# Two mixtures of experts in a decoder stack: the sorted blocks run as one pipeline over all parts

## The reference

```
# layer 0: the two best of eight experts, gated by silu
logits = x @ router_weight;  pick the 2 largest, weights from softmax
y = sum over the 2 picks of  weight * ((silu(x @ w1a[e]) * (x @ w1b[e])) @ w2[e])
x = layernorm(x + y)

# layer 1: one expert (best group of four, best expert of its two)
h = relu(x1 @ w1[e] + b1[e]);  y = combine * (h @ w2[e] + b2[e])
# then the layer's own norm with scale and bias, a residual, and the outer layernorm
```

## Time and profile before

| | us |
|---|---|
| median of the runs (three) | 4633.01 |
| the profiled execution | 4642.58 |
| its span, first to last instruction | 4640.8 |
| PE busy | 3776.7 (81%) |
| DVE busy | 3217.5 (69%) |
| ACT busy | 2241.0 (48%) |
| POOL busy | 1622.7 (35%) |
| mean granted TensorE clock | 0.897 of full |

### The profile page before, as it was taken

How to read it: one execution, slowest core, us unless ns; L and a number is a source line. 1 busy time by engine, 2 the same in 40 slices (tenths; PEclk the granted TensorE clock), 3 DMA queues, 4 the chain that set the end, 5 groups by cost and what they waited for, 6 DMA issues and landing times. The chain is left out here.

```text
span 4640.8 us, 137309 instructions
## 1 busy us (share of the span) xinstructions
PE 3776.7 (81%) x48696; PEld 2762.1 (60%) x48696; DVE 3217.5 (69%) x7860; ACT 2241.0 (48%) x4080; POOL 1622.7 (35%) x2677
## 2 busy tenths in 40 slices
PE   8997995268819999899998474898998968879986
PEld 6775664145517777677676352676775434447665
DVE  7986884233338888788796226788887767759985
ACT  4554551023424444466685133555784355545543
POOL 5653434603451111122354413233222234435543
PEclk9998995578969999999997687899999978889998
DMA  2011112165510000011001463000111100000001
GB/s 71 27 46 35 37 37 78 47 178 158 155 52 2 0 0 0 24 42 43 15 16 35 128 167 88 14 13 13 33 32 47 52 7 0 0 12 23 23 17 37
DMA packets 293801, 209.56 MB, mean 45 GB/s; under 512 B 51136, under 2 KB 272192, under 8 KB 293440
## 3 DMA queue, kind: packets, MB, share of 16 engines
q1 hardware_dynamic: 233760, 157.72, 11.9%
q0 software_dynamic: 12288, 25.19, 1.8%
q10 hardware_dynamic: 47520, 23.60, 1.7%
HBM read 122.49 MB, written 54.53 MB: 38 GB/s over the span
## 5 line engine op out<-in xcount | busy, mean ns | idle before, releaser
L955 POOL DMA_INDIRECT L0f_YG<-L0f_sorted_y,L0f_IDY x128 | 124.7, 974 | 214.8 <-DMA L0f_sorted_y<-L0f_YB 177.6
L1356 DVE TENSOR_TENSOR L0f_G<-L0f_SG,L0f_psH 128x512 f32<-128x512 f32 x106 | 73.0, 689 | 158.7 <-ACT L0f_SG L1098 95.2
L2219 POOL TENSOR_TENSOR L1a_rs<-L1a_ag,eps 128x1 f32<-128x1 f32 x64 | 12.3, 192 | 475.0 <-DVE L1a_ag L2379 475.0
L936 POOL DMA_INDIRECT L0f_sorted_x<-X,L0f_IDX x128 | 123.5, 965 | 86.7 <-DVE L0f_IDX L1202 48.6
L1029 PEld LDWEIGHTS L0f_psO<-L0f_WB,L0f_G 128*128 128x128 f32 x848 | 109.5, 199 | 57.1 <-issue 56.5
L1362 DVE TENSOR_TENSOR L1m_YB<-L1m_psO,L1m_WB 128x512 f32<-128x512 f32 x37 | 25.4, 687 | 170.4 <-PE L1m_psO L1029 115.6
L1029 PE MATMUL L0f_psO<-L0f_WB,L0f_G 128*128 128x128 f32 x848 | 111.6, 282 | 24.9 <-issue 24.6
L1022 PE MATMUL L1m_psH<-L1m_XT,L1m_WB 128*128 128x512 f32 x148 | 85.8, 709 | 55.8 <-ACT L1m_G L1101 40.0
L2306 PE MATMUL L1a_psO<-L1a_WO,L1a_OT 128*64 128x128 f32 x2048 | 125.9, 276 | 6.4 <-ACT L1a_OT L2330 5.0
L2240 PE MATMUL L1a_psF<-L1a_XT,L1a_WQ 128*128 128x256 f32 x512 | 130.1, 388 | 0.5 <-DVE L1a_KT L2195 0.5
L955 POOL DMA_INDIRECT L1m_YG<-L1m_sorted_y,L1m_IDY x64 | 62.7, 980 | 189.7 <-DMA L1m_sorted_y<-L1m_YB 148.1
(11 more groups left out here) (684 smaller groups left out, 12971.8 us busy)
## 6 DMA issues: line engine op xcount, KB each, us to landing
L0f_WB<-in_w12a SPq DMA_DIRECT2D x53, 312.0 KB
L0f_XB<-L0f_sorted_x SPq DMA_DIRECT2D x53, 256.0 KB
L0f_sorted_y<-L0f_YB ACTq DMA_DIRECT2D x53, 256.0 KB
L1m_WB<-in_w12b SPq DMA_DIRECT2D x37, 321.0 KB
L1m_XB<-L1m_sorted_x SPq DMA_DIRECT2D x37, 256.0 KB
L1m_sorted_y<-L1m_YB ACTq DMA_DIRECT2D x37, 256.0 KB
L0f_sorted_x<-L0f_AC SPq DMA_DIRECT2D x27, 256.0 KB, 2.6
L1m_sorted_x<-L1m_AC SPq DMA_DIRECT2D x27, 256.0 KB, 2.9
```

Of the source, the lines that this page charges most:

```text
L936: nc.gpsimd.indirect_dma_start(out=sorted_x[p][:, :], out_offset=bass.IndirectOffsetOnAxis(ap=IDX[:, k, t:t + 1], axis=0), in_=X[:, t, :], ...
L955: nc.gpsimd.indirect_dma_start(out=YG[:, b % 4, k, t % TB, :], out_offset=None, in_=sorted_y[p][:, :], in_offset=bass.IndirectOffsetOnAxis ...
L1356: nc.vector.tensor_tensor(G[0:f, J % 2, c, :], SG[0:f, c, :], up, ALU.mult).then_inc(S["g_ready"].sem, 1)
```

## The change

`PARTS` is set inside `routed_experts` and is 32, 16, 16 for layer 1 (blocks 15, 11, 11; still 37). The engines no longer empty the pipeline between parts: SP asks for rows(J+3) in every case, TensorE turns J+1 and does second(J−1) across the boundary, ScalarE likewise. The fills of part p+1 are issued one for each of the first eight blocks of part p. The side rows of batches 0 to 7 are asked for at every second block of part 1 (J = 15, 17, ..., 29) and worked on two blocks later (17 to 31); those of batches 8 to 15 come after the blocks, each behind a mixing step. The steps now stand so. Layer 0: 25:0, 27:1, 30:2, 32:3, 42:4, 44:5, 47:6, 49:7, 52:8, and eight after the blocks. Layer 1: 18:0, 20:1, 22:2, 24:3, 26:4, 28:5, 30:6, 32:7, 34:8, 36:9, and eight after.

```diff
-        PARTS = (16, 32, 16)
-
         def routed_experts(L, top, weights, router, bias=None, XO=None):
             gated, NE, GT = top == 2, 8, 16
+            PARTS = (16, 32, 16) if gated else (32, 16, 16)
...
-            step_after = {}
+            step_after, at = {}, 0
             for p in parts[1:]:
-                for k in range(PARTS[p - 1] // TB):
-                    at = first[p] + (4 + 2 * k if gated else 3 + 3 * k // 2)
-                    if at < first[p + 1]:
-                        step_after[at] = part_tile[p - 1] // TB + k
+                at = max(at, first[p] + ((10, 4)[p - 1] if gated else 3))
+                for b in range(part_tile[p - 1] // TB, part_tile[p] // TB):
+                    if at < BLOCKS:
+                        step_after[int(at)] = b
+                    at += 2.5 if gated else 2
+            SIDES = NBATCH // 2
...
-                    def fill(p):
+                    def fill(p, e):
                         made(sp, "prep", p + 1)
-                        for e in range(NE):
-                            last = sp.value_load(BT[0:1, p, 2, e:e + 1], min_val=0, max_val=ROWS - BATCH)
-                            sp.dma_start(rows_at(sorted_x[p], last), AC2[:, 0]).then_inc(S[f"filled{p}"].sem, 16)
-
-                    fill(0)
+                        last = sp.value_load(BT[0:1, p, 2, e:e + 1], min_val=0, max_val=ROWS - BATCH)
+                        sp.dma_start(rows_at(sorted_x[p], last), AC2[:, 0]).then_inc(S[f"filled{p}"].sem, 16)
+
+                    for e in range(NE):
+                        fill(0, e)
...
                     for J in range(BLOCKS):
-                        if J in (2, 6):
-                            fill((2, 6).index(J) + 1)
+                        p, k = part_of[J], J - first[part_of[J]]
+                        if p + 1 < len(PARTS) and k < NE:
+                            fill(p + 1, k)
                         if J + 3 < BLOCKS:
-                            if part_of[J + 3] == part_of[J]:
-                                rows(J + 3)
+                            rows(J + 3)
                             expert(J + 3)
-                        if J + 1 < BLOCKS and part_of[J + 1] != part_of[J]:
-                            for k in range(J + 1, J + 4):
-                                rows(k)
-                        if gated and J < NBATCH:
-                            side_rows(J)
+                        if gated and p == 1 and k % 2 == 0 and k // 2 < SIDES:
+                            side_rows(k // 2)
+                    if gated:
+                        for b in range(SIDES, NBATCH):
+                            side_rows(b)
...
                     for J in range(BLOCKS):
-                        if J + 1 < BLOCKS and part_of[J + 1] == part_of[J]:
+                        if J + 1 < BLOCKS:
                             turn_block(J + 1)
                         first_products(J)
-                        if J and part_of[J - 1] == part_of[J]:
+                        if J:
                             second(J - 1)
-                        if J + 1 == BLOCKS or part_of[J + 1] != part_of[J]:
-                            second(J)
-                            if J + 1 < BLOCKS:
-                                turn_block(J + 1)
+                    second(BLOCKS - 1)
...
-                            if J < NBATCH:
-                                side_work(J)
+                            k = J - first[1] - 2
+                            if k >= 0 and k % 2 == 0 and k // 2 < SIDES:
+                                side_work(k // 2)
...
+                    left = list(range(SIDES, NBATCH)) if gated else []
                     for b in range(done_steps, STEPS):
                         (tail_pair if gated else tail_one)(b)
+                        if left:
+                            side_work(left.pop(0))
+                    for b in left:
+                        side_work(b)
```

More of the change, by code:

```diff
@@ L1101, in _ @@
                                 nc.scalar.activation(G[:, J % 2, c, :], psH[:, c, :], ACT.Relu, bias=WB[:, J % 4, 512 + c:513 + c]).then_inc(S["g_ready"].sem, 1)
-                        if J and part_of[J - 1] == part_of[J]:
+                        if J:
                             out_and_store(J - 1)
-                        if J + 1 == BLOCKS or part_of[J + 1] != part_of[J]:
+                        if J + 1 == BLOCKS:
                             out_and_store(J)
-                            if J + 1 < BLOCKS:
-                                rows(J + 1)
                         if J in step_after and step_after[J]:
```

## The result

The changed kernel takes 4532.8 us (median; 4529.2 to 4533.7) against 4635.3 (4632.0 to 4642.2) for the kernel before on the same chip: ratio 0.9772, 95% interval 0.9757 to 0.9788, 102.5 us less. The profiled execution took 4532.05 us, its span is 4530.3 and its mean granted clock 0.904. The spans differ by 110.5, more than the medians, because the profiled execution of before was an upper one of its kernel.

What follows compares the result with a forecast made beforehand. Stalls between blocks bound it: VectorE waiting for context rows, TensorE for rows behind fills and at part boundaries, and long gather chains. Layer 0 −47.5 and layer 1 −37.9 sum to −85.4: median 4547 us, range 4500 to 4600.

Steps and rivals of the forecast that it cites:

- Layer 0, part 0: Layer 0's first part: VectorE's wait for context rows goes, 44.7 us too many becomes 5, −39.5.
- The 5 us that were to stay: Layer 0's first part: the restart at 934.7 (3 us) and some 2 us of contention remain.
- Boundaries, gathers and what is added: Layer 0, parts 1 and 2: boundaries −13, later gather chains −9, added DMA load +8, VectorE's mixing and side work +3.
- the −9 for the later gather chains: Layer 0: chains of eight no longer run into each other; half of 18 us drops, bounds 0 and −18.
- Contention (+8 and +6): DMA load and waits out of step: +8 in layer 0's blocks 15 to 22 (0 to 25), +6 in layer 1 (0 to 16).
- the side rows arrive late again: Rival: SP nearly full and DMA engines at their limit, eight stalls, two restarts, twice the contention, about 4596; chance 0.11.
- The tail of layer 0: After layer 0's last products: one mixing step fewer is finished, so gather batch 10 begins just after them, +3.
- Layer 1's blocks: Layer 1 without the start: fill stalls −20.4, boundaries −13.5, second gather chain −11, mixing steps −5, fill wait +2, DMA +6.
- The start of layer 1: Part 0's table comes some 25 us later, first rows about 2590 not 2565; ScalarE's late XT covers most, +4.
- The rival by which the DMA engines are never the bound: Fills hide wholly, 4533 from −14; if spaced gathers stop nobody but in the first chain, 4508; chance 0.14.
- The slower rival: Gathers inside both layers' blocks stop the pipeline for their whole length: were all lost, +126, 4673; chance 0.04.

Runs made afterwards that it cites:

- The single edits: Kernel before with one part of the change each: fills spread 4608.3 us, side rows and side work moved 4626.4, open pipeline 4625.4, layer 1's parts 4620.8.
- the other two: Kernel before with only the fills spread one per block (4608.3 us), and kernel before with only layer 1's parts 32, 16, 16 and their steps (4620.8 us).

## Why the prediction was right, and which term was not

The forecast was 4547 (−85.4 on the profile). Measured are 4532.8, and −110.2 between the same two ends of the profile. The difference of 24.8 is 17.6 in layer 1 up to its first YB, 4.6 ahead of layer 0's first store, by which two traces of one program also differ, and 2.6 in layer 0. So the mechanisms came as forecast, and the 4533 lies inside the range, but several terms were off and partly cancel; they are named below.

- **Layer 0, part 0: right.** −39.5 forecast, −40.1 measured. It rested on a subtraction (13 blocks at 4.80 against 107.1) and not on adding up the waits of the earlier trace rows, whose 25.3 us is little over half. The 5 us that were to stay are 4.5, in part by luck: 2.0 are the restart (6.8 us from store 1 to 2), no contention is seen (the intervals behind it are 4.80), and 2.5 are the part's last interval, which was 2.3 us before, when the pipeline was emptied there, and is a full 4.80 now. The single edits show the mechanism. On their chip part 0 takes 109.4 us with the layer 0 of before, 81.1 with the side work moved (VectorE's wait for the context rows falls from 93.0 on the first chip to 2.9), 103.4 with the fills spread and 107.6 with the open pipeline: −28, −6 and −2 of the 40.
- **Boundaries, gathers and what is added: right in sum, not term by term.** −11 forecast, −14.1 measured. Store to store over the two boundaries with their gather chains (14 to 20, 37 to 44) it is −11.9 and −12.4, so −24 where I had −13. The other intervals (20 to 37, 44 to 52) are +3.5 where I had +2 (−9 + 8 + 3): no contention is seen in them, and the −9 for the later gather chains isn't either. Another +6.7 is the end: before, the last products ended 7.4 us ahead of the last store, now 0.7.
- **Contention (+8 and +6): the load was there, the loss wasn't seen.** The changed kernel ahead of and behind part 1's first gather chain, while blocks 15 to 22 have rows, weights, a fill and side rows:

```profile
1003.00:1013.00 10.00, 9.79 (x54) 6.71 (x53) 3.60 (x13) 3.40 (x6) 7.56 (x9) 1.00 1.00 275
...
1037.00:1047.00 10.00, 10.00 (x54) 6.87 (x53) 4.70 (x15) 4.54 (x8) 0.00 (x0) 1.00 0.96 266
```

  The DMA engines are 0.96 to 1.00 busy at 266 to 275 GB/s, as the earlier trace rows let expect. Yet TensorE is busy 9.8 and 10.0 of 10 us, and in layer 1 the first blocks are, taken together, 1.5 us over their 3.94 each (stores 2 to 6). Rows asked for three blocks ahead have 14 us to come in, which I take for the reason. The Trainium skill (DMA: Bandwidth & Descriptors, section Bandwidth) gives 435 GB/s as the fabric's ceiling; the trace stays far below that with the engines 0.96 to 1.00 busy. Of the forecast's 14 us of contention no more than 1.5 are seen.
- **Side work: right, and dear where it is wrong.** The rival "the side rows arrive late again" had 29 + 6 us without contention for eight stalls. Asked for in the same block they cost 44.
- **The tail of layer 0: right** (+3 forecast, +4.1 measured). Batch 10's gather, at 1281.12 in the earlier trace rows, begins at 1228.73, 4.4 us after the last products, behind a root that waited for the mixing step of block 52:

```profile
1227.22 0.19 POOL L943 TENSOR_TENSOR L0f_rt<-L0f_ag,eps 128x4 f32<-128x4 f32 x1 [12.01 <-ACT X L1079]
...
1228.73 1.00 POOL L956 DMA_INDIRECT L0f_YG<-L0f_sorted_y,L0f_IDY  x1 [0.19 <-issue]
```

- **Layer 1's blocks: right, and to the microsecond by luck.** −41.9 forecast without the start, −42.0 measured (−44.6 + 2.6). Against 3.94 us a block, the two intervals behind the fills were 21.3 us too long and are 0 now; those at the boundaries with their gather chains went from 41.3 to 14.9, those with mixing steps alone from 17.8 to 11.6. That is −53.9 where −49.9 had been forecast. Of the +6 for contention no more than 1.5 are seen; but 8.0 us of the slow start now lie behind the first YB. One long stall is left, in the one chain of 16 gathers, as forecast: 12.31 us, in the place of two.

```profile
2657.34 3.75 PE L1023 MATMUL L1m_psH<-L1m_XT,L1m_WB 128*128 128x512 f32 x4 [12.31 <-ACT L1m_G L1099]
```

- **The start of layer 1: wrong, by 17.6 us at the first YB and 9.5 at the third store.** The step read: "The start: part 0's table now comes with the second scatter chain ... which covers most: **+4** (−4 to +20)". The table does come later, and the eight fills do take 21.36 us of SP inside a scatter chain; but the first block is turned as early as before (77.1 us after the router's first product, 76.8 in the kernel before), and the first YB comes 13.6 us earlier. The second YB then comes late (12.8 us after the first, 3.9 before), so 5.5 us of the lead are left at the third store, where +4 had been forecast. I had only asked whether SP would be late, and had taken the 16.48 us for which ScalarE was held in the earlier trace rows as a fixed cover. ScalarE's timeline in the changed kernel:

```profile
2552.10 1.09 ACT L1058 ACTIVATE L1m_XT<-L1m_psX 128x512 f32<-128x512 f32 x2 [15.00 <-remote]
2554.86 0.69 ACT L1099 ACTIVATE L1m_G<-L1m_psH,L1m_WB 128x512 f32<-128x512 f32 x1 [1.68 <-PE L1m_psH L1023]
2556.57 0.69 ACT L1099 ACTIVATE L1m_G<-L1m_psH,L1m_WB 128x512 f32<-128x512 f32 x1 [1.02 <-issue]
...
2567.09 0.60 ACT L1058 ACTIVATE L1m_XT<-L1m_psX 128x512 f32<-128x512 f32 x1 [6.61 <-PE L1m_psX L1005]
```

  ScalarE wakes at 2552.10 and gets two XT and four G done before it is held again, which is where the second block loses time. POOL's timeline there:

```profile
2548.29 0.96 POOL L937 DMA_INDIRECT L1m_sorted_x<-X,L1m_IDX  x1 [0.30 <-issue]
2553.61 0.96 POOL L937 DMA_INDIRECT L1m_sorted_x<-X,L1m_IDX  x1 [4.36 <-DVE L1m_IDX L1198]
```

  It wakes in the gap between the third and the fourth scatter chain, 4.36 us here. In the kernel before, the same gap is 1.52 us:

```profile
2603.55 0.96 POOL L936 DMA_INDIRECT L1m_sorted_x<-X,L1m_IDX  x1 [0.30 <-issue]
2606.03 0.96 POOL L936 DMA_INDIRECT L1m_sorted_x<-X,L1m_IDX  x1 [1.52 <-issue]
```

```profile
2609.40 0.60 ACT L1060 ACTIVATE L1m_XT<-L1m_psX 128x512 f32<-128x512 f32 x1 [16.48 <-remote]
2616.51 0.60 ACT L1060 ACTIVATE L1m_XT<-L1m_psX 128x512 f32<-128x512 f32 x1 [6.51 <-remote]
2620.71 0.69 ACT L1101 ACTIVATE L1m_G<-L1m_psH,L1m_WB 128x512 f32<-128x512 f32 x1 [3.60 <-remote]
```

  There ScalarE works through the same items one by one, held for 3.5 to 6.5 us before each. The short gap and the slow start (37 us) go together in the kernel before and in the two kernels with the side work moved and the open pipeline; the long gap and the fast start (23 to 24) in the other two and the changed one. The second traces agree: under 0.6 us and 37.8 in the kernel before, 4.33 and 21.4 in the changed one. That pauses of POOL can release the others is shown in layer 0 by the pauses in the scatters (73 us); that this gap does it here is read from the times and from these eight traces, and no run sets the gap alone. Why VectorE's last group of IDX comes earlier in the kernels with the short gap, when the fills are bunched and the parts old, is not settled.

The rival by which the DMA engines are never the bound (4533, given 0.14) has the measured time, and on contention it was right, by the stretches above: no more than 1.5 of the 14 us are seen. That the time agrees so well is luck all the same, since the start, the boundaries, the later chains and the end of layer 0's blocks were off by 7 to 11 us each, in both directions. The slower rival (gathers stop the pipeline throughout) didn't come: parts 1 and 2 of layer 0, with 80 gathers beside them, are 44 us over their steady time (132.7 − 23 × 4.80 and 94.0 − 15 × 4.80), where 59 were over before.

## What to carry to other kernels

Take the excess of a pipeline from its steady step (blocks times 4.80 us against the stretch), then look for the waits behind it: that sum came within 1 us for layer 0's first part, where the waits alone gave a little over half. In an in-order queue, here SP's, a burst of eight issues costs what it holds back (10 us, a stall of 8 to 11) and one per step cost nothing that is seen. VectorE needed its context rows asked for two blocks ahead: in the same block they cost 44 us. Measure an early start some steps further on: of 13 us at the first block's output 4 to 6 were left at the third. Before a kernel is rearranged around a stall, measure on more than one chip whether the stall is there.

## What the hardware showed that I had not expected

- **Long chains of indirect DMAs on POOL all but stop TensorE, VectorE and ScalarE, on some chips only.** Same program, same chain (1.26 us each): TensorE busy 6.6 of 80 us on one chip, 71.1 of 80 on another. Of five comparisons three met it (before 4635 to 4651 us), two did not (4399 to 4401; one of the two by the time of before alone).
- **A pause ends it, for a while.** Waiting for landing after each eight scatters, 1.5 us, brought 71 us (ratio 0.962, the best measured on a chip with the standstill); six blocks beside such chains still took 10.7 to 14.2 us. On a chip without it, pauses after each four, in the gathers too, cost some 112 us against the worked-out time of the changed kernel. No version beats the changed kernel on both kinds in these runs: the pauses per eight weren't run on a chip without the standstill.
- **One program, two clocks.** Layer 1's last 16 blocks are the same program in four kernels' traces on the chips without the standstill, apart from gathers paced otherwise ahead of them in two: 70.7 and 72.8 us at a granted clock of 1.00, 80.1 and 79.7 at 0.91. A difference of under 10 us in one trace need not come from the edit.
- What the other engines lack while they stand still isn't shown; the trace puts most of it to "issue" and "remote". The Trainium skill (Runtime: NRT & Kernel Launch, section Instruction fetch mechanics) says that engines fetch their instructions by DMA and that this is mostly hidden. Two such packets are in the trace of the changed kernel between 785 and 870 us, both before 805, and none from there to 895; on the chip without the standstill seven are. Whether the chains hold fetches back, or the idle engines just ask for none, these runs don't show.
